# A decoder layer on one core: the projections' 64-row group as 128 high-and-low columns in four passes

## The chip, the cores and the metric

The kernel runs on one core of a Trainium2 chip. The metric is the device time of one execution in microseconds. Engines: TensorE (PE in the profile, its weight load PEld), VectorE (DVE), ScalarE (ACT), GpSimd (POOL), SyncE (SP, which here issues all DMAs).

## The reference, cut to what matters

Four batches of 1024 tokens with 256 features go through a linear attention of rank 64, a cross attention and a feed-forward network in a 4-bit grid. The change lies in the first of them:

```python
Q = x @ WQ.T;  K = x @ WK.T;  invQ = Q @ Winv.T;  invK = K @ Winv.T
z = jnp.cumsum(x, axis=1) / counts
fwd_r = Q @ V_b * jnp.cumsum(K @ W_b, axis=1)
inv_r = jnp.cumsum(invK @ V_b, axis=1) * (invQ @ W_b)
tri_r = Q @ V_t * jnp.cumsum(K @ W_t, axis=1) * (z @ X_t)
out = (fwd_r @ U_b.T + 0.5 * inv_r @ U_b.T + 0.5 * tri_r @ U_t.T + biases) / counts
```

## The kernel before

Products in full precision are made of two parts of each factor: a high part (rounded, type fp32r) and a low part (the rest). `mm_parts` (L1031 to L1033) makes three matmuls of them: high by high, high by low, low by high.

The 256x256 weights are folded into seven column groups of R = 64 in the preparation: `proj_h` and `proj_l` are [128, 2, 7 * 64]. The columns 6R to 7R are those of invQ @ W_b. A half batch of 512 tokens (`q` = 0 to 7) is projected by `proj_tiles`: groups t = 0, 1, 2 give 128 rows each, t = 3 gives 64. Each has two contraction steps `k`, so 6 matmuls of 512 columns. Group 0 and 2 go to PSUM bank 6, groups 1 and 3 to bank 7 (other banks in the preparation).

VectorE takes them: `bi_half` (L1535 and the scan L1528) for groups 0 and 1, and `tri_half` for groups 2 and 3. `tri_half` scans group 2, multiplies its lower 64 rows with group 3 (L1543, which reads PSUM), the upper 64 with the inverse counts (L1545), and adds or multiplies both into `ranks` (L1548, L1550). `y_half` (L1149) multiplies `ranks` with the output weights, and `x1_half` (L1558) adds that to X.

The order on every engine is written out by hand; engines wait for one another by counting semaphores. `s_proj` counts the groups that TensorE made, `s_proj_used` what VectorE took of them, `s_tri` the finished `ranks`. After a preparation (up to about 51 us), which also projects batch 0, the function `batch(b, more)` runs for b = 0 to 3: it does the cross attention of batch b in steps i = 0 to 9 (tiles of 128 queries), and with `more` (b = 0 to 2) the linear attention of batch b + 1 between them. On TensorE step i = 3 projects groups 0 and 1 of the first half of b + 1, i = 4 groups 2 and 3, i = 5 makes the output product and turns the second normed half, i = 6 projects its groups 0 and 1, i = 7 its groups 2 and 3, i = 8 makes the second output product. In i = 4 VectorE has the maximum of tile 4, `tri_half`, two `gate_tile` (gz, L1574), `raw_scales` (for the feed-forward weights) and `mix_tile` of tile 2; in i = 5 the maximum of tile 5, `x1_half`, `mix_tile` of tile 3, `raw_rounder`, and `xnT_low` (the low half of the turned normed input, L1498), which the projections of i = 6 wait for. `mix_tile` makes dmix (L1590), which frees the PSUM bank of the next PV product (`pv_tile`, L1228 and L1230). In i = 7 VectorE has `tri_half`, `mix_tile` of tile 5 and, for b = 0 and 1, the statistics of two batches ahead. GpSimd's operations in these steps are additions and products of SBUF tiles: `bias_half` (L486), `sum_half` (L502), `base_tiles` (L509, L513) and those on the raw weights, which first wait for VectorE's `wsc`. Then a loop over 32 tiles does the feed-forward network.

## Time and profile before

| | us |
|---|---|
| median of three runs | 545.34 (544.75 to 546.62) |
| the profiled execution | 544.99 |
| its span | 543.2 |
| PE busy | 523.3 (96%) |
| PEld busy | 455.9 (84%) |
| DVE busy | 449.6 (83%) |
| ACT busy | 343.2 (63%) |
| POOL busy | 409.6 (75%) |

The profile is one execution. Busy time is a sum of instructions; matmuls overlap each other, so their step from start to start says more than their duration. The views used are the page (parts by number), the timeline (instructions of one engine in order of time; in brackets how long the engine stood idle before it and what ended that), groups by source line, and windows (busy time of each engine in a stretch, with TensorE's granted clock as a share of full speed).

### The profile page before, as it was taken

The numbers are of one execution on the slowest core, as the hardware profiler recorded it, in microseconds if no ns is written. First come the engines' busy times: TensorE is split into PE (matmuls) and PEld (weight loads), VectorE is DVE, ScalarE is ACT, GpSimd is POOL, SyncE is SP. The second block draws the span as 40 slices with busy tenths as digits, with TensorE's granted clock in tenths as the row PEclk, the third lists the DMA queues.
The fourth block names the chain that finished last, engine by engine and source line by source line (L and its number), as shares of the span: only waits on it lengthen the run. The fifth ranks groups of instructions, "written<-read, shape, count | busy, mean of one in ns | idle before, by whom it ended". The sixth has DMA issues, their size and how long they took to land.

```text
span 543.2 us, 10677 instructions
## 1 busy us (share of the span) xinstructions
PE 523.3 (96%) x3089; PEld 455.9 (84%) x3089; DVE 449.6 (83%) x1118; ACT 343.2 (63%) x811; POOL 409.6 (75%) x639
## 2 busy tenths in 40 slices
PE   7998899999999999999999998999999999999997
PEld 4876688888888888888888887898899999999996
DVE  3688579786797957978679779998899999999986
ACT  3555544747446266553486666887778888888763
POOL 4156938949769499498796938889988888888864
PEclk9998999999999999999999999999999999999999
DMA  8621300000000000000000000000000000000001
GB/s 245 190 89 48 113 1 1 1 2 1 1 1 0 2 1 1 2 0 2 1 2 1 0 1 1 1 19 20 19 20 20 19 19 19 20 24 24 21 19 49
DMA packets 16130, 13.86 MB, mean 26 GB/s; under 512 B 3883, under 2 KB 15839, under 8 KB 16095
## 3 DMA queue, kind: packets, MB, share of 16 engines
q1 hardware_dynamic: 16095, 13.43, 8.1%
q8 instruction: 17, 0.28, 0.2%
q14 instruction: 18, 0.15, 0.1%
HBM read 9.23 MB, written 4.19 MB: 25 GB/s over the span
## 4 chain that ended last, share of the span: by engine, by line
PE 70%; DVE 15%; issue 7%; ACT 5%; POOL 2%; DVEq 0%; ACTq 0%; POOLq 0%
PE ps L1031 16%; PE ps L1033 15%; PE ps L1032 15%; PE ps L1230 10%; PE ps L1410 3%; PE ps L1218 2%; PE ps L1228 2%; ACT xn_sums L714 1%; PE ps L1149 1%; DVE X L1558 1%; DVE gz L1574 1%; PE ps L1278 1%; PE ps L1121 1%; DVE parts L1498 1%; DVE st L1562 1%
## 5 line engine op out<-in xcount | busy, mean ns | idle before, releaser
L1031 PE MATMUL ps<-keys_h,nT_h 128*128 128x256 f32 (+6 forms) x272 | 85.9, 316 | 2.7 <-DVE keys_l L1498 1.9
L1033 PE MATMUL ps<-keys_h,nT_l 128*128 128x256 f32 (+6 forms) x272 | 83.1, 306 | 0.0
L1032 PE MATMUL ps<-keys_l,nT_h 128*128 128x256 f32 (+6 forms) x272 | 83.1, 306 | 0.0
L1031 PE MATMUL ps<-parts,xq_parts 128*128 128x512 f32 (+1 forms) x192 | 74.5, 388 | 0.0
L1033 PE MATMUL ps<-parts,xq_parts 128*128 128x512 f32 (+1 forms) x192 | 72.0, 375 | 0.0
L1032 PE MATMUL ps<-parts,xq_parts 128*128 128x512 f32 (+1 forms) x192 | 71.7, 373 | 0.0
L1230 PE MATMUL ps<-V,probT 128*128 128x256 f32 x288 | 67.4, 379 | 0.0
L757 ACT ACTIVATE prob<-ps,nbias 128x205 f32<-128x205 f32 (+7 forms) x32 | 25.7, 804 | 60.7 <-DVE nbias L1580 60.6
L1230 PEld LDWEIGHTS ps<-V,probT 128*128 128x128 f32 x288 | 54.5, 189 | 7.7
L1031 PEld LDWEIGHTS ps<-keys_h,nT_h 128*128 128x128 f32 x272 | 51.3, 188 | 7.1 <-DVE keys_l L1498 2.3
L1032 PEld LDWEIGHTS ps<-keys_l,nT_h 128*128 128x128 f32 x272 | 51.4, 189 | 3.3
L631 POOL TENSOR_TENSOR probT<-prob,probT 128x704 f32<-128x704 f32 x31 | 47.5, 1533 | 8.3 <-ACT probT L831 8.3
L1033 PEld LDWEIGHTS ps<-keys_h,nT_l 128*128 128x128 f32 x272 | 51.4, 189 | 1.6
L633 POOL TENSOR_TENSOR probT<-probT 128x704 f32<-128x704 f32 x31 | 47.7, 1540 | 2.4
L520 POOL TENSOR_TENSOR pool_carrier<-powers 128x1 f32<-128x1 f32 x70 | 15.0, 214 | 45.4 <-DVE wsc L1615 27.8
L1696 DVE TENSOR_TENSOR prob<-prob,ps 128x256 f32<-128x256 f32 (+1 forms) x96 | 37.6, 393 | 12.6 <-ACT prob L815 12.4
L829 ACT ACTIVATE probT<-prob 128x704 bf16<-128x704 f32 x31 | 24.5, 791 | 28.4 <-DVE prob L1715 28.3
L1580 DVE TENSOR_REDUCE nbias<-ps 128x1 f32<-128x205 f32 (+7 forms) x32 | 26.4, 826 | 17.5 <-PE ps L1202 17.5
L1498 DVE TENSOR_TENSOR nT_l<-ps,nT_h 128x768 fp32r<-128x768 f32 (+2 forms) x49 | 40.7, 845 | 0.1
L1033 PEld LDWEIGHTS ps<-parts,xq_parts 128*128 128x128 f32 x192 | 36.0, 188 | 5.4
L1032 PEld LDWEIGHTS ps<-parts,xq_parts 128*128 128x128 f32 x192 | 36.2, 188 | 4.6
L1031 PEld LDWEIGHTS ps<-parts,xq_parts 128*128 128x128 f32 x192 | 36.1, 188 | 4.3
(236 smaller groups left out, 1595.4 us busy)
## 6 DMA issues: line engine op xcount, KB each, us to landing
X<-in_x_dram SPq DMA_DIRECT2D x8, 512.0 KB, 4.4
out_dram<-X SPq DMA_DIRECT2D x32, 128.0 KB, 1.7
early<-in_L_ffn_w_down_dram SPq DMA_DIRECT2D x1, 704.0 KB, 6.7
early<-in_L_ffn_w_gate_dram SPq DMA_DIRECT2D x1, 640.0 KB, 4.5
early<-in_L_ffn_w_up_dram SPq DMA_DIRECT2D x1, 640.0 KB, 5.7
ctx_rows<-in_ctx_dram SPq DMA_DIRECT2D x1, 308.0 KB
early<-in_L_attn_Winv_dram SPq DMA_DIRECT2D x1, 256.0 KB, 3.9
early<-in_L_attn_WQ_dram SPq DMA_DIRECT2D x1, 256.0 KB, 4.6
```

What stands on the lines that cost most here:

```text
L631: g.tensor_tensor(ht, hy, hm, ALU.add).then_inc(s_h_added, 1)
L633: g.tensor_tensor(ht, ht, hm, ALU.subtract).then_inc(s_h_rounded, 1)
L757: a.activation(prob[:, i % 2, CTX0:L], flat[:, CTX0:L], ACT.Exp, bias=nbias[:, i:i + 1], scale=1.0, accum_out=rsum[:, i:i + 1]).then_inc(s ...
L829: a.activation(hsq, hy, ACT.Square, scale=GRID_SLOPE).then_inc(s_hsq, 1)
L1031: mm(o, wh, mh, start=start, stop=False, **kw)
L1032: mm(o, wh, ml, start=False, stop=False, **kw)
L1033: return mm(o, wl, mh, start=False, stop=stop, **kw)
L1230: last = mm(ps[:, 5, 0:D], probT[:, i % 2, m, :], V[:, m - 1, :], start=False, stop=(m == i + 1))
L1410: last = turn(ps[:, 5 + k // 4, (k % 4) * P:(k % 4 + 1) * P], hq_wide[:, k * P:(k + 1) * P], ident[:])
L1498: return v.tensor_tensor(o, whole, high.bitcast(F32), ALU.subtract)
L1580: v.tensor_reduce(nbias[:, i:i + 1], flat[:, CTX0:(i + 2) * P], AX.X, ALU.max, negate=True).then_inc(s_neg_max, 1)
L1696: v.tensor_tensor(hh[:, lo:lo + width], sg[:, lo:lo + width], ps[:, c, width:2 * width], ALU.mult).then_inc(s_hh, 1)
```

## The change

In the preparation the low part of the seventh column group is written behind its high part, as an eighth group of `proj_h`. For t = 3 TensorE then makes, in each of the two contraction steps, one matmul with these 128 columns (high and low) and the high part of the input, into 128 rows of the bank, and one with the 64 high columns and the low part of the input, added into the lower 64 rows: four matmuls in place of six. ScalarE copies the upper 64 rows to a new tile `inv_q` (`inv_q_low`, called at i = 4 and 7 and twice in the preparation), VectorE adds the lower 64 rows to it, and L1543's operation reads `inv_q` in place of PSUM. Two semaphores are new. In `tri_half` the product with the inverse counts now comes ahead of these.

```diff
--- before.py
+++ after.py
@@ -119,6 +119,7 @@
         fwd_tri = sb("fwd_tri", [P, HTOK])
         inv_z = sb("inv_z", [P, HTOK])
         ranks = sb("ranks", [P, S])
+        inv_q = sb("inv_q", [R, HTOK])
         st2 = sb("st2", [P, HALF, 6])
         mv2 = sb("mv2", [P, TPB, 2])
         sm = sb("sm", [P, 11, TPB])
@@ -180,7 +181,7 @@
 
 
 
-        xnT_h, xnT_l, proj_h, proj_l, att_h, att_l = rooms(parts, HTOK, HTOK, 7 * R, 7 * R, D, D)
+        xnT_h, xnT_l, proj_h, proj_l, att_h, att_l = rooms(parts, HTOK, HTOK, 8 * R, 7 * R, D, D)
         gwT_h, gwT_l = rooms(xq_parts, D, D)
 
         xn1 = hid[:, HALF:TPB, :]
@@ -269,6 +270,8 @@
         s_proj_used = sem("proj_used")
         s_zE = sem("zE")
         s_tri = sem("tri")
+        s_inv_q = sem("inv_q")
+        s_inv_q_sum = sem("inv_q_sum")
         s_biased = sem("biased_input")
         s_att_w = sem("attention_weights")
 
@@ -740,6 +743,13 @@
                                         scale=sm[:, 1, i:i + 1])
                 last.then_inc(s_hid, 1)
 
+            def inv_q_low(q, bank=6):
+
+                act.wait_ge(s_proj, q * 4 + 4)
+                if not (isinstance(q, int) and q == 0):
+                    act.wait_ge(s_inv_q_sum, q)
+                a.activation(inv_q[:], ps[R:2 * R, bank + 1, :], ACT.Copy).then_inc(s_inv_q, 1)
+
             def gate_tile(b, i):
                 act.wait_ge(s_gz, b * TPB + (i + 1))
                 act.wait_ge(s_base, b * TPB + (i + 1))
@@ -836,6 +846,8 @@
                         exp_tile(b, i)
                     if 1 <= i <= TPB:
                         turn_tile(b, i - 1)
+                    if more and i in (4, 7):
+                        inv_q_low(b * 2 + (2 + i // 7))
                     if more and i in (2, 5):
                         xnT_half(b * 2 + (2 + i // 5), i // 5)
                     if i == (1 if is_first(b) else 0):
@@ -910,6 +922,7 @@
                 act.wait_ge(s_xn_turned, 2 + (j + 1))
                 a.activation(xnT1_h[:, :, j * 2 * P:(j + 1) * 2 * P],
                              ps[:, j, :].rearrange("p (k n) -> p k n", k=KD), ACT.Copy).then_inc(s_xnT_h, 1)
+            inv_q_low(0, 4)
             act.wait_ge(prep_mm, 4)
             a.activation(out_w[:], ps[:, 2, 0:D], ACT.Copy)
             a.activation(bias_row[:], ps[:, 2, D:2 * D], ACT.Copy).then_inc(prep_ev, 1)
@@ -924,6 +937,7 @@
             last.then_inc(s_att_w, 1)
             act.wait_ge(prep_mm, 7)
             a.activation(gwT_h, ps[:, 2, :].rearrange("p (j n) -> p j n", j=KD), ACT.Copy).then_inc(prep_ev, 1)
+            inv_q_low(1, 4)
             norm2_half(0, 0)
             act.wait_ge(prep_mm, 8)
             for m in range(KD):
@@ -1129,11 +1143,17 @@
                         pe.wait_ge(s_xnT_l, q * 2 + 2)
                     if t >= 2 and banks[0] == banks[2]:
                         pe.wait_ge(s_proj_used, q * 4 + (t - 1))
-                    m = R if t == 3 else P
                     for k in range(KD):
-                        c = slice(t * P, t * P + m)
-                        last = mm_parts(ps[0:m, banks[t], :], (proj_h[:, k, c], proj_l[:, k, c]),
-                                        (xT[0][:, k, :], xT[1][:, k, :]), start=(k == 0), stop=(k == KD - 1))
+                        c = slice(t * P, (t + 1) * P)
+                        if t < 3:
+                            last = mm_parts(ps[:, banks[t], :], (proj_h[:, k, c], proj_l[:, k, c]),
+                                            (xT[0][:, k, :], xT[1][:, k, :]), start=(k == 0), stop=(k == KD - 1))
+                        else:
+
+                            mm(ps[:, banks[t], :], proj_h[:, k, c], xT[0][:, k, :], start=(k == 0), stop=False,
+                               skip_group_check=True)
+                            last = mm(ps[0:R, banks[t], :], proj_h[:, k, 6 * R:7 * R], xT[1][:, k, :], start=False,
+                                      stop=(k == KD - 1), skip_group_check=True)
                     last.then_inc(s_proj, 1)
 
             def y_half(b, h):
@@ -1538,12 +1558,14 @@
 
                 c = slice(h * HTOK, (h + 1) * HTOK)
                 scan(q, h, scan_rest, bank, 3)
-                ve.wait_ge(s_proj, q * 4 + 4)
                 ve.wait_ge(s_proj_used, q * 4 + 3)
-                v.scalar_tensor_tensor(inv_z[0:R, :], scan_rest[0:R, :], alphas[0:R, 0:1], ps[0:R, bank + 1, :], ALU.mult,
-                                       ALU.mult).then_inc(s_proj_used, 1)
                 v.tensor_tensor(inv_z[R:2 * R, :], scan_rest[R:2 * R, :], inv_row[R:2 * R, c], ALU.mult).then_inc(s_zE, 1)
+                ve.wait_ge(s_inv_q, q + 1)
+                v.tensor_tensor(inv_q[:], ps[0:R, bank + 1, :], inv_q[:], ALU.add).then_inc(s_proj_used, 1)
                 ve.wait_ge(s_proj_used, q * 4 + 4)
+                v.scalar_tensor_tensor(inv_z[0:R, :], scan_rest[0:R, :], alphas[0:R, 0:1], inv_q[:], ALU.mult,
+                                       ALU.mult).then_inc(s_inv_q_sum, 1)
+                ve.wait_ge(s_inv_q_sum, q + 1)
                 ve.wait_ge(s_y, b * TPB)
                 v.tensor_tensor(ranks[0:R, c], fwd_tri[0:R, :], inv_z[0:R, :], ALU.add)
                 ve.wait_ge(s_zE, q + 1)
@@ -1829,8 +1851,8 @@
             ve.wait_ge(prep_ev, 1)
             for m in range(KD):
                 low(pairs_of(proj_l[:, m, 0:4 * R]), bilinear_sums(m), pairs_of(proj_h[:, m, 0:4 * R]))
-                low(pairs_of(proj_l[:, m, 3 * R:7 * R])[:, :, R:2 * R], trilinear_sums(m),
-                    pairs_of(proj_h[:, m, 3 * R:7 * R])[:, :, R:2 * R])
+            low(proj_l[:, :, 4 * R:5 * R], ps[:, 0:KD, 2 * R:3 * R], proj_h[:, :, 4 * R:5 * R])
+            low(proj_h[:, :, 7 * R:8 * R], ps[:, 0:KD, 5 * R:6 * R], proj_h[:, :, 6 * R:7 * R])
             low(proj_l[:, :, 5 * R:6 * R], xt[:], proj_h[:, :, 5 * R:6 * R]).then_inc(prep_v, 1)
             ve.wait_ge(w_in[2], 16 * 7)
             v.tensor_scalar(ub2[:, :, R:2 * R], ut[:], alphas[:, 1:2], None, ALU.mult)
```

## Rows read from the trace of the kernel before

**Rows 1.** Page, part 4: the chain that ended last, share of the span by engine.

```profile
PE 70%; DVE 15%; issue 7%; ACT 5%; POOL 2%; DVEq 0%; ACTq 0%; POOLq 0%
```

**Rows 2.** Timeline of PE, batch 0, first half (start us, us, engine line op tiles).

```profile
75.22 0.40 PE L1031 MATMUL ps<-parts 128*64 128x512 f32 x1
...
76.61 0.28 PE L1031 MATMUL ps<-xq_parts,nT_h 128*128 128x256 f32 x1
```

**Rows 3.** Timeline of DVE, same stretch, tri_half and what follows.

```profile
75.42 1.22 DVE L1528 TENSOR_TENSOR_SCAN xn_sums<-ones,ps 128x512 f32<-128x512 f32 x1 [1.04 <-PE ps L1033]
76.81 0.74 DVE L1543 SCALAR_TENSOR_TENSOR inv_z<-xn_sums,alphas,ps 64x512 f32<-64x512 f32 x1 [0.16 <-PE ps L1033]
77.58 0.69 DVE L1545 TENSOR_TENSOR inv_z<-xn_sums,inv_row 64x512 f32<-64x512 f32 x1
78.30 0.68 DVE L1548 TENSOR_TENSOR ranks<-fwd_tri,inv_z 64x512 f32<-64x512 f32 x1
79.72 0.88 DVE L1574 SCALAR_TENSOR_TENSOR gz<-ps,sm,gate_row 128x256 f32<-128x256 f32 x2
```

**Rows 4.** Timeline of DVE, low half of the next normed input.

```profile
91.93 1.28 DVE L1498 TENSOR_TENSOR parts<-ps,parts 128x512 fp32r<-128x512 f32 x2
```

**Rows 5.** Timeline of PE, the two places that follow VectorE in the first half.

```profile
87.17 1.06 PE L1121 MATMUL ps<-ident,xn_sums 128*128 128x128 f32 x8 [0.29 <-DVE X L1558]
...
92.86 0.28 PE L1033 MATMUL ps<-xq_parts,nT_l 128*128 128x256 f32 x1
...
93.26 0.50 PE L1031 MATMUL ps<-parts 128*128 128x512 f32 x1
```

**Rows 6.** Timeline of PE, batch 0, second half: PV product of tile 7.

```profile
119.16 0.60 PE L1228 MATMUL ps<-ctx_rows,probT 77*128 77x256 f32 x2
```

**Rows 7.** Timeline of DVE, batch 0, second half: tri_half's end, dmix of tile 6.

```profile
107.44 1.10 DVE L1548 TENSOR_TENSOR ranks<-fwd_tri,inv_z 64x512 f32<-64x512 f32 x1
...
108.55 1.27 DVE L1550 TENSOR_TENSOR ranks<-fwd_tri,inv_z 64x512 f32<-64x512 f32 x1
...
118.33 0.48 DVE L1590 SCALAR_TENSOR_TENSOR dmix<-ps,rinv,th 128x256 f32<-128x256 f32 x1
```

**Rows 8.** Timelines of DVE and PE, the same two places in batch 2.

```profile
258.66 0.48 DVE L1590 SCALAR_TENSOR_TENSOR dmix<-ps,rinv,th 128x256 f32<-128x256 f32 x1
...
261.19 0.60 PE L1228 MATMUL ps<-ctx_rows,probT 77*128 77x256 f32 x2
```

**Rows 9.** By source line: ScalarE's 64-row copy, VectorE's L1676 (ns min/median/max).

```profile
L906 ACT ACTIVATE inv_row<-ps x2: 582/588/595, 17.2 to 17.7; 64x512 f32<-64x512 f32 x2
L1676 DVE SCALAR_TENSOR_TENSOR nrm<-nrm,ps x29: 406/408/414, 320.7 to 509.4; 128x256 f32<-128x256 f32 x29
L1676 DVE SCALAR_TENSOR_TENSOR nrm<-nrm,xs x3: 620/817/936, 281.8 to 303.4; 128x256 f32<-128x256 f32 x3
```

**Rows 10.** Timeline of POOL, batch 0, first half.

```profile
82.86 0.19 POOL L520 TENSOR_TENSOR pool_carrier<-powers 128x1 f32<-128x1 f32 x1 [8.66 <-DVE wsc L1615]
```

**Rows 11.** Timeline of POOL, batch 0, second half.

```profile
108.54 1.86 POOL L513 TENSOR_TENSOR X<-X,hid 128x256 f32 x2
```

**Rows 12.** Timelines of DVE, POOL and PE in the preparation, in order of time.

```profile
25.45 0.69 DVE L1550 TENSOR_TENSOR ranks<-fwd_tri,inv_z 64x512 f32<-64x512 f32 x1
...
25.72 0.47 POOL L520 TENSOR_TENSOR pool_carrier<-powers 128x1 f32<-128x1 f32 x1 [13.79 <-ACT bias_row L915]
...
27.09 1.89 PE L1149 MATMUL ps<-out_w,ranks 128*128 128x256 f32 x8
...
32.88 0.69 DVE L1498 TENSOR_TENSOR xq_parts<-ps,xq_parts 128x512 fp32r<-128x512 f32 x1 [0.40 <-ACT xq_parts L926]
...
51.47 0.42 PE L1031 MATMUL ps<-keys_h,nT_h 128*128 128x334 f32 x1 [0.82 <-ACT prob L757]
```

**Rows 13.** Windows of 1 us: busy of each engine, then PEclk, DMA share, GB/s.

```profile
45.00:46.00 1.00, 0.00 (x0) 0.00 (x0) 1.00 (x6) 0.39 (x1) 0.77 (x4) 1.00 0.00 0
...
47.00:48.00 1.00, 1.00 (x7) 0.95 (x7) 0.96 (x5) 0.76 (x3) 0.99 (x2) 0.54 0.09 16
```

## The prediction

> **What bounds the kernel now.** I read the views in this order. First the page's chain of work that ended last [rows 1]: TensorE carries 70% of it, VectorE 15%. So the kernel is near TensorE's limit, but a sixth of the end is set by VectorE, and the question is whether the edited step lies in that sixth. Then the timelines around the 64-row group. In batch 0 the six 64-row matmuls run from 75.22 to 76.61 [rows 2]: 1.39 / 6 = 0.232 us from start to start. VectorE meanwhile scans group 2, which it had waited for, and then does four dependent 64x512 operations [rows 3]; the step from L1545 to L1548, both from SBUF alone, is 78.30 - 77.58 = 0.72 us. From that scan on, VectorE has no idle time up to the end of the next low half of the normed input, 91.93 + 1.28 = 93.21 [rows 4], and TensorE starts the next projections 0.05 us later, at 93.26 [rows 5]. Its last gate matmul began at 92.86, and one of 256 columns takes 0.12 us from start to start (estimated as half of 0.232), so it was free at 92.98 and stood 0.28 us; at 87.17 it stood for VectorE too, for X of L1558 [rows 5]. Batches 1 and 2 repeat this pattern, so it stands three times in the trace. Thus the first half of each `more` batch is set by VectorE from group 2's end on. The second half is different: there the next place where TensorE needs VectorE is the PV product of tile 7, at 119.16 [rows 6], which needs dmix of tile 6, done at 118.33 + 0.48 = 118.81 [rows 7]; slack 0.35, less 0.05 for the signal. Batch 2's second half has more: 258.66 + 0.48 = 259.14 against 261.19 [rows 8], because two batches ahead there is nothing left to norm.
>
> **The change part by part.**
>
> TensorE. Two of six matmuls go in each of eight half batches, 16 x 0.232 = 3.7 us [rows 2], and group 3 ends 0.46 us earlier each time. Group 2's end does not move. That four passes cost four times 0.232, although half of them load 128 columns and half 64, is read from the same rows: 128- and 64-column matmuls follow each other without a longer step. What the trace does not show is a switch at every pass; its bounds are 0 and one more step of 0.232 per group, and I take 0 since both switches of the present group show nothing; even 0.232 would be hidden where VectorE decides. The Trainium skill, TensorEngine Tiling (Array Packing), Key Properties, says that a change of tiling mode drains the engine; if a 64-column pass counts as such a mode, that speaks against the change, but the present switches show no drain, and by either the sum stays within the bounds just given.
>
> ScalarE. A 64x512 copy from PSUM takes 582 to 595 ns [rows 9], so 8 x 0.59 = 4.7 us. It waits for group 3, at i = 4 and 7. Queued behind it at i = 4 are the tanh of tiles 4 and 5, which need gate products that TensorE makes after group 3 anyway; at i = 7 it is the turning copy of tile 7, likewise made later. In the preparation the second copy stands ahead of norm2_half(0, 0), and who needs that one's turned output is VectorE's nT_low, queued behind the second tri_half, which waits for the same copy. Cost 0 in these places. Is the copy in time for VectorE's add? The old L1543 began at 76.81; group 3 now ends 0.46 before that, 76.35, the copy at 76.94, and the add is due only after L1545, at 76.81 + 0.72 = 77.53. Yes, by 0.6 us. In the second half ScalarE is still copying tile 6 then, and I allow 0.1 us.
>
> VectorE. The product L1545 goes first, then comes the new add (PSUM and SBUF, 64x512), then L1543's operation with both tensors in SBUF, then L1548 and L1550. One more dependent operation: I take 0.72 us by L1545's step; the other end is 0.77, the step 76.81 to 77.58 [rows 3]. The low halves of the weights in the preparation change their slices, not their number or element count: 0.
>
> First halves, batches 0 to 2: VectorE's run from the scan to 93.21 is 0.72 longer, and TensorE's start at 93.26 moves by all of it; its own 0.46 only lengthens its standing. GpSimd is idle meanwhile (8.66 us until wsc, [rows 10]), so nothing is slowed. 3 x 0.72 = +2.2.
>
> Second halves, batches 0 and 1: here GpSimd's X minus hid runs beside VectorE from 108.54 [rows 11], and L1548 and L1550, both with two SBUF sources, take 1.10 and 1.27 us [rows 7] where L1545 took 0.69 [rows 3]. With L1543 reading SBUF only, there are three such operations in the stretch; GpSimd ends at 110.40, so the last one is relieved. I take 0.72 + 0.1 (copy) + 0.2 (contention) = 1.0. dmix then ends at 119.8, TensorE's PV at 119.86: +0.7 each, +1.4. Bounds 0.4 (0.72 alone: 118.81 + 0.72 + 0.05 - 119.16) and 1.1 each. Batch 2: 259.14 + 1.0 is before 261.19 - 0.46 = 260.73, so here the saving counts: -0.46.
>
> Preparation, two half batches. VectorE ended L1550 at 25.45 + 0.69 = 26.14 and TensorE began the output product L1149 at 27.09 [rows 12], busy up to then. Now TensorE arrives at 26.63, VectorE at 26.86. But GpSimd's bias additions wait for bias_row, which comes 0.46 after fewer matmuls, so they start at 25.72 - 0.46 = 25.26 and run beside L1548 and L1550, which now lie 0.72 later (25.47 on). By [rows 7] against [rows 3] that adds 0.4 + 0.6 = 1.0: output product at 27.9, +0.84. From there TensorE runs through to the turned gate weights; ScalarE copies them, and VectorE's low half waits for that copy at 32.88 [rows 12]. From 32.88 VectorE is busy with no idle time until the first maximum, whose exponential TensorE waits for at 51.47 [rows 12]; in that run lies the second tri_half, +0.72. Together +1.5; without contention 26.86 + 0.05 - 27.09 + 0.72 = +0.5. I take 1.5, since all four GpSimd additions fall in the stretch.
>
> Batch 3 and the feed-forward loop have no edited step and shift as a whole. Sum: 1.5 + 2.2 + 1.4 - 0.5 = +4.6 us. Against the profiled execution, 544.99, that is 549.6; the median of the three runs lies 0.35 above it, so 549.9. With the low ends 0.5 + 2.2 + 0.8 - 0.5 = +3.0 (548.3), with the high ends 1.6 + 2.3 + 2.2 - 0.2 = +5.9 (551.2).
>
> **The rivals.**
>
> (a) TensorE sets everything and VectorE's 0.72 is absorbed: -3.7, 541.6. For it: TensorE's share of the chain [rows 1]. Against it: the idle-free VectorE run that ends 0.05 us before TensorE's start, in all three batches, and the standing at 87.17.
>
> (b) Only the first halves and the preparation lose, and in the second halves the chain to dmix of tile 6 has more room than I read (from an order of waits that the records don't show): 0.5 + 2.2 - 3 x 0.46 = +1.3, 546.6. It decides where VectorE gains more than 0.7 us before 118.33.
>
> (c) L1543's operation becomes slow since both its sources now lie in SBUF. Nearest rows: L1676, 128x256, 408 ns with one source in PSUM and 620 to 936 ns with both in SBUF [rows 9]. Taking the lowest, +0.21 for 256 columns, +0.42 for 512, at seven places where VectorE decides: +2.9, 552.8. Against it: those three ran beside GpSimd's operations, as L1548 did. The Trainium skill, Vector Engine (DVE) Microarchitecture Reference, Points that are easy to get wrong, says that such an operation with two SBUF sources that aren't bf16 runs at half rate; this would be the same mechanism. No row shows it undisturbed.
>
> (d) The clock. At 45 to 46 TensorE is not busy at all, and at 47 to 48 its granted clock is 0.54, towards the 1.2 GHz level [rows 13]; VectorE's run hides that now. TensorE's standing before the second output product (about 40 us) grows by about 0.7. If the clock falls there already, the 12 matmuls of 512 columns for the keys take 0.232 more each, +2.8: 552.7.
>
> (e) The saving does not come, since the fused pass takes longer or the sequence stays at six steps: then VectorE's part is the same and batch 2 loses its -0.46: 550.4, inside the range.
>
> **How the numbers follow.** About 0.3%, 1.6 us, is what a measurement of this kernel can tell from no change, so "same" is 543.7 to 547.0. My sum, with (e) in it, has 0.62; (a) 0.08, (b) 0.12, (c) 0.12, (d) 0.06. Faster is (a), 0.08; same is (b), 0.12; slower is the rest, 0.80. The predicted time is 549.9. The range goes down to (b) and up to (c) and (d), 546.4 to 552.9, which leaves out (a) and the outer ends of (c) and (d), no more than 2 in 10.
>
> **What would show it.** TensorE's group 3 in four matmuls, next work 0.46 us sooner after group 2. VectorE from the scan's start to that of gz, L1574, 79.72 - 75.42 = 4.3 us before [rows 3], now 5.0 in first halves. TensorE standing before the turns of the normed input and before the projections 0 and 1 in every first half, longer by 0.7 to 1.2. In second halves a new standing before the PV product of tile 7, named as waiting for dmix, in batches 0 and 1 and not in 2. The first exponential's follower at about 53.0 rather than 51.47. The forecast is wrong if the stretch from group 2's end to the next projections has the same length as before, or if L1543's operation, undisturbed, takes over 0.8 us.

## The result, and the profile after

| | before | after |
|---|---|---|
| median | 545.14 (544.75 to 546.62, 4 runs) | 551.29 (549.80 to 551.39, 4 runs) |
| the profiled execution | 544.99 | 551.25 |
| its span | 543.2 | 549.5 |
| PE busy | 523.3 (96%) | 521.0 (95%) |
| DVE busy | 449.6 (83%) | 456.7 (83%) |
| ACT busy | 343.2 (63%) | 347.9 (63%) |

The changed kernel is slower: ratio 1.0093, 95% interval 1.0071 to 1.0115, which is 3.9 to 6.3 us. Predicted were 549.9 us with a range of 546.4 to 552.9. The executions of either kernel lie in groups some 1.5 us apart (the kernel before on another chip: 8 of 19 runs at 544.96 to 545.44, the others at 546.51 to 548.11). Of the four runs above, one of the kernel before lies above its lower group and three of the changed one do, so the 6.15 us between the medians hold some luck; what the groups come from is taken up at the end of the experiments.

The lines of `tri_half` have new numbers: scan L1548, the product with the inverse counts L1562, the new addition L1564, L1543's operation L1566, the two rank operations L1570 and L1572, dmix L1612. The fused passes are L1153 and L1155, `mm_parts` L1045 to L1047, the output product L1169, the turns of the normed input L1135.

The page of after, part 4 (the chain that ended last, as [rows 1]):

```profile
PE 59%; DVE 22%; issue 8%; ACT 8%; POOL 1%; DVEq 0%; ACTq 0%; POOLq 0%
```

TensorE's share fell from 70% to 59%, VectorE's rose from 15% to 22%: work was taken from the engine that mostly sets the end and given to one that sets it in places. Where it does so is in the view of TensorE's waits between 62 and 345 us (line that waited, what for: us in total, times, longest). Before:

```profile
PE ps L1121 <- DVE X L1558: 0.9, 3, 0.3
PE ps L1031 <- DVE gz L1574: 0.5, 1, 0.5
```

and after:

```profile
PE ps L1135 <- DVE X L1580: 4.1, 3, 1.4
PE ps L1248 <- DVE dmix L1612: 1.5, 2, 0.8
PE ps L1045 <- DVE gz L1596: 1.0, 3, 0.5
```

The first line is the standing before the turns of the normed input, once in every first half (0.3 us each before, 1.4 now). The second did not exist before: the PV product of tile 7 waits for dmix of tile 6, in two batches of three.

How far the second trace runs behind the first can be followed by the starts of the 32 PV products, L1228 before and L1248 after. The delay is 2.31 us at the first one (62.62 to 64.93), so the preparation gave this. From tile 1 of one batch to tile 1 of the next it grows to 3.97, 5.65 and 6.12 us; within batch 3 it stays at 6.12 to 6.13. Split at tile 4, the three first halves gave 0.62, 0.58 and 0.57 us, the second halves 1.03, 1.10 and -0.10.

**TensorE's part came as forecast.** Timeline of PE of after, batch 0, first half, and further on the turns:

```profile
77.55 0.40 PE L1153 MATMUL ps<-parts 128*128 128x512 f32 x1
77.79 0.39 PE L1155 MATMUL ps<-parts 128*64 128x512 f32 x1
78.02 0.39 PE L1153 MATMUL ps<-parts 128*128 128x512 f32 x1
78.24 0.39 PE L1155 MATMUL ps<-parts 128*64 128x512 f32 x1
...
90.09 1.06 PE L1135 MATMUL ps<-ident,xn_sums 128*128 128x128 f32 x8 [1.35 <-DVE X L1580]
```

Four passes in place of six, 0.22 to 0.24 us from start to start, with 128 and 64 columns in turn and nothing between them. The 0.46 us saved reappear at L1135 as standing, 1.35 us in place of the 0.29 of [rows 5].

**VectorE, undisturbed.** Timeline of DVE of after, same stretch, to be held against [rows 3]:

```profile
77.75 1.22 DVE L1548 TENSOR_TENSOR_SCAN xn_sums<-ones,ps 128x512 f32<-128x512 f32 x1 [1.04 <-PE ps L1047]
79.01 0.69 DVE L1562 TENSOR_TENSOR inv_z<-xn_sums,inv_row 64x512 f32<-64x512 f32 x1
79.73 0.68 DVE L1564 TENSOR_TENSOR inv_q<-ps,inv_q 64x512 f32<-64x512 f32 x1
80.45 0.74 DVE L1566 SCALAR_TENSOR_TENSOR inv_z<-xn_sums,alphas,inv_q 64x512 f32<-64x512 f32 x1
81.22 0.68 DVE L1570 TENSOR_TENSOR ranks<-fwd_tri,inv_z 64x512 f32<-64x512 f32 x1
81.92 0.69 DVE L1572 TENSOR_TENSOR ranks<-fwd_tri,inv_z 64x512 f32<-64x512 f32 x1
82.64 0.88 DVE L1596 SCALAR_TENSOR_TENSOR gz<-ps,sm,gate_row 128x256 f32<-128x256 f32 x2
```

From the scan to gz it is 82.64 - 77.75 = 4.89 us, before it was 4.30.

**VectorE beside GpSimd.** The second half of batch 0, as [rows 7]; first DVE, then POOL, then the PE product that waits:

```profile
108.80 0.77 DVE L1562 TENSOR_TENSOR inv_z<-xn_sums,inv_row 64x512 f32<-64x512 f32 x1
109.68 0.68 DVE L1564 TENSOR_TENSOR inv_q<-ps,inv_q 64x512 f32<-64x512 f32 x1
110.40 0.98 DVE L1566 SCALAR_TENSOR_TENSOR inv_z<-xn_sums,alphas,inv_q 64x512 f32<-64x512 f32 x1
111.42 1.25 DVE L1570 TENSOR_TENSOR ranks<-fwd_tri,inv_z 64x512 f32<-64x512 f32 x1
112.69 1.14 DVE L1572 TENSOR_TENSOR ranks<-fwd_tri,inv_z 64x512 f32<-64x512 f32 x1
...
122.35 0.48 DVE L1612 SCALAR_TENSOR_TENSOR dmix<-ps,rinv,th 128x256 f32<-128x256 f32 x1
```

```profile
108.98 1.86 POOL L512 TENSOR_TENSOR hid<-hid,th 128x256 f32<-128x256 f32 x2
...
111.39 1.88 POOL L516 TENSOR_TENSOR X<-X,hid 128x256 f32 x2
```

```profile
122.89 0.70 PE L1248 MATMUL ps<-ctx_rows,probT 77*128 77x256 f32 x2 [0.76 <-DVE dmix L1612]
```

The same three operations that took 0.74, 0.68 and 0.69 us take 0.98, 1.25 and 1.14 here. The addition, which has one source in PSUM, keeps its 0.68.

**The preparation.** Windows of after around the first logits (us, busy time and count of PE, PEld, DVE, ACT, POOL, then TensorE's granted clock, DMA share, GB/s):

```profile
48.00:49.00 1.00, 1.00 (x11) 0.99 (x10) 0.96 (x10) 1.00 (x3) 1.00 (x2) 1.00 0.06 16
...
51.00:52.00 1.00, 0.00 (x0) 0.00 (x0) 1.00 (x5) 0.43 (x3) 0.92 (x3) 1.00 0.00 0
...
53.00:54.00 1.00, 1.00 (x6) 0.77 (x5) 0.00 (x0) 0.75 (x2) 1.00 (x2) 0.50 0.51 160
54.00:55.00 1.00, 1.00 (x4) 0.47 (x4) 0.51 (x1) 0.43 (x1) 1.00 (x3) 0.50 1.09 388
```

and of before:

```profile
48.00:49.00 1.00, 1.00 (x6) 1.00 (x7) 1.00 (x10) 1.00 (x3) 0.84 (x6) 0.50 0.00 0
...
53.00:54.00 1.00, 1.00 (x9) 0.79 (x8) 0.27 (x1) 0.81 (x5) 1.00 (x2) 1.00 1.07 376
54.00:55.00 1.00, 1.00 (x11) 1.00 (x10) 0.00 (x0) 1.00 (x4) 1.00 (x3) 1.00 1.11 342
```

In both traces TensorE has a stretch of 3 to 4 us at the lower level, 1.2 GHz (0.50). Before, it lay at 47 to 51 us, where TensorE is early and VectorE's run decides. After, it lies at 52 to 56 us, in the logits of tile 1 and the turns behind them, which TensorE alone sets. Their start came 52.15 - 51.47 = 0.68 us later. This execution had begun a little sooner, though: VectorE's first low half of the projection weights (called the first low half below) starts at 14.92 and not at 15.14, so from there it is 37.23 us against 36.33, and the change made the way 0.90 us longer. From the logits to the first PV product it is 64.93 - 52.15 = 12.78 us against 62.62 - 51.47 = 11.15, so in this pair of executions the clock costs 1.63 us.

### The profile page after: what moved, and what is told of

Same layout as the page of the kernel before. It is cut to its first block, busy times and chain, and to the rows that moved or that the text cites. A ratio compares the mean times of both kernels' runs of the same rounds, so it can differ in the third digit from the quotient of the medians.

```text
span 549.5 us, 10660 instructions
## 1 busy us (share of the span) xinstructions
PE 521.0 (95%) x3073; PEld 454.1 (83%) x3073; DVE 456.7 (83%) x1126; ACT 347.9 (63%) x819; POOL 410.3 (75%) x639
## 4 chain that ended last, share of the span: by engine, by line
PE 59%; DVE 22%; issue 8%; ACT 8%; POOL 1%; DVEq 0%; ACTq 0%; POOLq 0%
PE ps L1045 13%; PE ps L1047 13%; PE ps L1046 13%; PE ps L1250 6%; PE ps L1430 3%; DVE X L1580 2%; ACT xn_sums L717 1%; DVE st L1509 1%; PE ps L1248 1%; DVE xn_sums L1548 1%; PE ps L1238 1%; DVE st L1584 1%; DVE nT_l L1518 1%; DVE dmix L1612 1%; DVE nbias L1602 1%
## 5 line engine op out<-in xcount | busy, mean ns | idle before, releaser
L1045 PE MATMUL ps<-keys_h,nT_h 128*128 128x256 f32 (+6 forms) x272 | 86.1, 316 | 4.3 <-ACT prob L767 2.4
L1047 PE MATMUL ps<-keys_h,nT_l 128*128 128x256 f32 (+6 forms) x272 | 83.4, 307 | 0.0
L1045 PE MATMUL ps<-parts,xq_parts 128*128 128x512 f32 (+1 forms) x192 | 74.6, 388 | 0.0
L1047 PE MATMUL ps<-parts,xq_parts 128*128 128x512 f32 (+1 forms) x192 | 72.0, 375 | 0.0
L1045 PEld LDWEIGHTS ps<-keys_h,nT_h 128*128 128x128 f32 x272 | 51.5, 189 | 8.6 <-ACT prob L767 2.6
L1047 PEld LDWEIGHTS ps<-keys_h,nT_l 128*128 128x128 f32 x272 | 51.5, 189 | 1.7
L1718 DVE TENSOR_TENSOR prob<-prob,ps 128x256 f32<-128x256 f32 (+1 forms) x96 | 37.6, 392 | 12.7 <-ACT prob L825 12.5
L1047 PEld LDWEIGHTS ps<-parts,xq_parts 128*128 128x128 f32 x192 | 36.0, 188 | 5.4
L1045 PEld LDWEIGHTS ps<-parts,xq_parts 128*128 128x128 f32 x192 | 36.2, 188 | 4.3
```

The lines of the kernel that those rows point to most:

```text
L1045: mm(o, wh, mh, start=start, stop=False, **kw)
L1047: return mm(o, wl, mh, start=False, stop=stop, **kw)
L1718: v.tensor_tensor(hh[:, lo:lo + width], sg[:, lo:lo + width], ps[:, c, width:2 * width], ALU.mult).then_inc(s_hh, 1)
```

## The experiments

My theory after the two traces: (1) the addition makes VectorE's run longer by 0.6 us at each half, (2) in second halves three operations with both sources in SBUF are stretched by GpSimd's work, (3) in the preparation 0.7 us is VectorE's and 1.6 us the place of the low-clock stretch, (4) TensorE's saving is worth nothing where VectorE decides. The rivals: the loss is in the fused passes or the copy; operations with two SBUF sources are slow in any case; TensorE's shorter group is a gain that something else eats.

The ratios in this part stand against runs of the kernel before made in between on the same chip; its median there was 546.54 (19 runs) for the first four kernels, 546.67 (26 runs) for the next four and 545.38 (17 runs) for the last two.

**The clock.** The changed kernel, with eight matmuls of no use behind the first two gate products of batch 0:

```diff
+                    if i == 0 and is_first(b):
+                        keep_warm(8, 5)
```

> The changed kernel with eight 512-column bf16 matmuls of identity by identity (their result is not read, they fill the bank of the PV products) in step 0 of batch 0, behind the gate products of tiles 0 and 1, where TensorE stood 2.38 us. Theory (the clock fell in that standing and the next 3.5 us ran at the 1.2 GHz level, which cost 2.31 - 0.68 = 1.6 us): 549.6, the PV product of tile 0 of batch 0 begins at about 63.3 instead of 64.93, and the granted clock from 52 to 56 us is 1.00. Rival (the 1.6 us come from later waits for ScalarE or VectorE, the low clock is only seen beside them): 551.2, the PV product stays at 64.9.

Measured: 550.63 us (550.20 to 551.44, 4 runs), ratio 1.0079 (1.0047 to 1.0110). The profiled run (550.54) had the granted clock 1.00 in every window from 40 to 66 us, and from the first logits to the first PV product it took 64.27 - 53.12 = 11.15 us, as before. That logits start at 53.12 and not at 52.15 is not the edit's: this execution was 0.97 us late already at VectorE's first low half, 15.89 against 14.92 us. So the 1.63 us between the two profiles are the clock's. The runs don't show a gain: the interval overlaps that of the changed kernel (1.0071 to 1.0115), and the two medians, 0.66 us apart, belong to series in which the kernel before had 545.14 and 546.54. An execution starts earlier or later by up to 1 us, and the last section shows that the stretch does not fall on the same matmuls in each.

**The saving alone.** The kernel before with four passes, no copy and no addition; the low part of the weights is left out of invQ @ W_b:

```diff
-                    m = R if t == 3 else P
...
+                            mm(ps[:, banks[t], :], proj_h[:, k, c], xT[0][:, k, :], start=(k == 0), stop=False,
+                               skip_group_check=True)
+                            last = mm(ps[0:R, banks[t], :], proj_h[:, k, 6 * R:7 * R], xT[1][:, k, :], start=False,
+                                      stop=(k == KD - 1), skip_group_check=True)
```

> TensorE's part alone: the 64-row group in four passes, but no copy and no add, VectorE takes the lower 64 rows from PSUM as before; the product of the group's low weights with the input is left out of the result. Theory: nothing is gained in the three first halves, where VectorE decides; 0.46 in the preparation, 0.46 in the second half of batch 2, at most 0.30 in those of batches 0 and 1: -1.5 us, 543.6. Rival (TensorE sets everything): -3.7, 541.4.

Measured: 545.69 us (543.88 to 547.25, 10 runs), ratio 0.9984 (0.9967 to 1.0002), that is -1.8 to +0.1 us: the rival's -3.7 is out, the forecast -1.5 is not. The profiled run had a low clock twice, at 52 to 57 and 59 to 64 us (2.99 us late at the first PV product), so the trace is read from there: the delay falls to 2.28 us at the end, -0.71 in all, and -0.41 of that is batch 2's second half. In the first halves it falls by 0.46 and comes back by 0.39; TensorE's waits tell where:

```profile
PE ps L1121 <- DVE X L1564: 2.1, 3, 0.7
```

Against 0.9 us before: of each 0.46 us saved in the group, 0.4 us is now standing for X. So of the 2.8 us of work that the six half batches behind the preparation save, 0.7 comes through, most of it where VectorE is not late. In the preparation the saving shows once more: from the first low half to the first logits it is 35.89 us against 36.33.

**The addition alone.** Six passes as before, ScalarE's copy multiplied by zero, and the addition:

```diff
-                a.activation(inv_q[:], ps[R:2 * R, bank + 1, :], ACT.Copy).then_inc(s_inv_q, 1)
+                a.activation(inv_q[:], ps[0:R, bank + 1, :], ACT.Copy, scale=0.0).then_inc(s_inv_q, 1)
```

> ScalarE's and VectorE's part alone: TensorE makes the 64-row group in six passes as before; ScalarE copies its 64 rows times zero to inv_q and VectorE adds that, so every added instruction and wait of the change is there. Theory (VectorE sets the first halves and, for the longer tri_half, the second ones too, so TensorE's saving is worth little beside it): 551.2 to 552.0, at most 0.7 us above the changed kernel. Rival (the saving of 16 x 0.232 = 3.7 us was had in full and the rest cost over 9 us): 555.0.

Measured: 551.90 us (550.18 to 553.30, 4 runs), ratio 1.0089 (1.0055 to 1.0123), which can't be told from the changed kernel's. The profiled run (553.30) had a granted clock of 0.50 from 54 to 57 us and 0.72 on the mean of 60 to 66. From its first PV product on, the first halves give 0.60 us each (4.12 to 4.72, 5.84 to 6.44, 7.55 to 8.14), the second halves 1.12, 1.10 and 0. So the loss in the halves needs no fused pass; it is the copy's and the addition's.

**GpSimd's share.** The changed kernel, with `base_tiles` of tiles 6 and 7 held back until `tri_half` of the second half is done:

```diff
+                if more:
+                    pool.wait_ge(s_tri, b * 2 + 4)
```

> The changed kernel with one wait more: in the second halves GpSimd begins the products and subtractions of tiles 6 and 7 only when VectorE has finished tri_half, so they don't run beside it. Theory (contention for SBUF stretched the three operations with two SBUF sources to 0.98, 1.25 and 1.14 us): they take 0.74, 0.68 and 0.69 us, 1.26 less; TensorE's standing before the PV product of tile 7 goes, about -1.1 us each in batches 0 and 1, -0.4 in batch 2: 548.6. Rival (they are slow for another reason, such as two SBUF sources by themselves): their durations stay, and the added wait costs up to 1 us: 551.2 to 552.5.

Measured: 547.77 us (546.97 to 549.05, 10 runs), ratio 1.0031 (1.0013 to 1.0049). Timeline of DVE and of POOL, batch 0, second half (lines here are two higher than in after):

```profile
109.87 0.68 DVE L1566 TENSOR_TENSOR inv_q<-ps,inv_q 64x512 f32<-64x512 f32 x1
110.59 0.74 DVE L1568 SCALAR_TENSOR_TENSOR inv_z<-xn_sums,alphas,inv_q 64x512 f32<-64x512 f32 x1
111.37 0.68 DVE L1572 TENSOR_TENSOR ranks<-fwd_tri,inv_z 64x512 f32<-64x512 f32 x1
112.07 0.69 DVE L1574 TENSOR_TENSOR ranks<-fwd_tri,inv_z 64x512 f32<-64x512 f32 x1
```

```profile
112.92 1.61 POOL L512 TENSOR_TENSOR hid<-hid,th 128x256 f32<-128x256 f32 x2 [3.67 <-DVE ranks L1574]
```

All three are back at their undisturbed times, and the second halves cost -0.17, -0.13 and -0.44 us (read by the PV products) in place of 1.03, 1.10 and -0.10. The first halves stay at 0.57. One wait takes 2.8 us off the three second halves. That is more than the change lost there, for the kernel before has contention in them too, and no run holds GpSimd back in it. The Trainium skill says in GPSIMD Engine Reference, Specifications, that GpSimd shares its SBUF interfaces with VectorE and that they collide in instructions of VectorE with two SBUF inputs; this trace agrees, with 0.98 against 0.74, 1.25 against 0.68 and 1.14 against 0.69 us.

**Two sources in SBUF or one.** The changed kernel, the sum written to PSUM:

```diff
-                v.tensor_tensor(inv_q[:], ps[0:R, bank + 1, :], inv_q[:], ALU.add).then_inc(s_proj_used, 1)
+                v.tensor_tensor(ps[0:R, bank + 1, :], ps[0:R, bank + 1, :], inv_q[:], ALU.add).then_inc(s_proj_used, 1)
```

> The changed kernel with one edit: VectorE's addition writes the sum back into the group's bank of PSUM, so that the operation behind it (the alphas' multiply and add, L1566) has one source in SBUF again, as in the kernel before. Theory (operations with both sources in SBUF are stretched while GpSimd works, and only then): undisturbed nothing changes, 0.74 us for L1566 either way; in the second halves of batches 0 and 1, where L1566 took 0.98 us beside GpSimd, it takes 0.74 to 0.77, while the two rank operations behind it stay above 1.1 us. That is 2 x 0.24 = 0.5 us: 550.8 us. Rival (L1566 lasts longer for the mere order of work, or VectorE's second source from PSUM is as exposed as one from SBUF): L1566 stays at 0.95 or more in second halves, 551.3 us.

Measured: 549.49 us (547.97 to 551.12, 10 runs), ratio 1.0044 (1.0027 to 1.0061). Timeline of DVE and of POOL, batch 0, second half:

```profile
110.64 0.74 DVE L1566 SCALAR_TENSOR_TENSOR inv_z<-xn_sums,alphas,ps 64x512 f32<-64x512 f32 x1
111.42 0.68 DVE L1570 TENSOR_TENSOR ranks<-fwd_tri,inv_z 64x512 f32<-64x512 f32 x1
112.11 1.12 DVE L1572 TENSOR_TENSOR ranks<-fwd_tri,inv_z 64x512 f32<-64x512 f32 x1
```

```profile
111.60 2.23 POOL L516 TENSOR_TENSOR X<-X,hid 128x256 f32 x2 [0.15 <-issue]
```

L1566 took 0.74 us beside GpSimd, as the theory had it; that L1570 would stay above 1.1 us was wrong. Since L1566 was done sooner, L1570 had begun before GpSimd's next operation (111.42 against 111.60), and now GpSimd's was the one stretched: 2.23 us for two in place of 1.88. So the profiled gain was 0.24 + 0.57 us in this half, 0.8 where 0.24 was forecast. Undisturbed, in the first half, the operation takes 0.74 us with both sources in SBUF (after) and 0.74 us with one in PSUM (before and here).

**Moving the upper rows to GpSimd.** GpSimd makes the two products of the upper 64 rows (L1545 and L1550) in batches 1 to 3, first in the kernel before, then in the changed one, then with the extra matmuls too:

```diff
+                pool.wait_ge(s_proj_used, q * 4 + 3)
+                g.tensor_tensor(inv_z[R:2 * R, :], scan_rest[R:2 * R, :], inv_row[R:2 * R, c], ALU.mult).then_inc(s_zE, 1)
...
+                g.tensor_tensor(ranks[R:2 * R, c], fwd_tri[R:2 * R, :], inv_z[R:2 * R, :], ALU.mult).then_inc(s_upper, 1)
```

> The kernel before with GpSimd making the upper 64 rows' two products (L1545 and L1550) in batches 1 to 3, and everything else as it was. VectorE's run of a first half gets 1.4 us shorter. Theory (in the kernel before, TensorE stands only 0.28 and 0.45 us for VectorE in a first half, and nearly nothing in a second): a first half gives back at most 0.7 us, three of them 2.1, and the second halves give nothing or lose some tenths, since GpSimd was working there anyway: 543.5 us, between 542.8 and 545. Rival (VectorE's run sets the halves in full, so that what it loses comes back in full): 6 x 1.4 = 8 us, 537. Second rival (GpSimd is slower at these products and VectorE waits for it at the next half): 546 or more.

Measured: 543.95 us (542.22 to 545.39, 6 runs), ratio 0.9952 (0.9925 to 0.9978), the one kernel here that beats both. In its trace the delay to the kernel before goes from -0.04 to -0.98, -1.89 and -2.79 us: each first half gives 0.9 us, more than the 0.73 us of standing that I had counted, and each second half nothing.

> The changed kernel with the same edit: GpSimd makes the upper 64 rows' two products (L1562 and L1572) in batches 1 to 3. That takes 1.4 us from a VectorE run that the change made 0.6 us longer. Theory (the change loses by VectorE's run at every half, and TensorE's shorter group shows once that run is covered): first halves go from +0.6 to about -0.45 against the kernel before, second halves from +1.1 to about -0.45; the preparation's 2.3 us stay, for batch 0 is not touched: 545.1 + 2.3 - 3 x 0.45 - 3 x 0.45 = 544.7 us; with a share of the second halves lost to GpSimd, up to 546.5. Rival (the loss sits in TensorE or in the copy, not in VectorE's length): 551 us. Second rival (GpSimd takes over as what ends last): above 549.

Measured: 549.83 us (548.29 to 551.37, 9 runs), ratio 1.0054 (1.0036 to 1.0072), where 544.7 to 546.5 were expected. A miss, and the timelines of DVE and POOL in the first half tell why:

```profile
78.05 0.68 DVE L1590 TENSOR_TENSOR inv_q<-ps,inv_q 64x512 f32<-64x512 f32 x1 [0.40 <-ACT inv_q L771]
78.77 0.79 DVE L1592 SCALAR_TENSOR_TENSOR inv_z<-xn_sums,alphas,inv_q 64x512 f32<-64x512 f32 x1
79.59 1.65 DVE L1596 TENSOR_TENSOR ranks<-fwd_tri,inv_z 64x512 f32<-64x512 f32 x1
```

```profile
77.73 1.28 POOL L529 TENSOR_TENSOR inv_z<-xn_sums,inv_row 64x512 f32<-64x512 f32 x1 [2.53 <-DVE xn_sums L1570]
79.17 1.53 POOL L532 TENSOR_TENSOR ranks<-fwd_tri,inv_z 64x512 f32<-64x512 f32 x1 [0.15 <-POOL inv_z L529]
```

Of the 1.4 us taken from VectorE, 0.40 is spent standing for ScalarE's copy, which the product L1562 had covered, and 0.97 on L1596, which runs beside GpSimd's product and takes 1.65 us in place of 0.68. The first halves gave 0.52, 0.49 and 0.55 us, nearly as in after, the second ones 0.49, 0.55 and -0.44. I had counted GpSimd's idle time as free, and left out that the edit itself ends it at the moment VectorE's two-source operation runs. In the kernel before the same edit had L1548's operation at 0.98 us, not 1.65, and no copy to wait for.

> The kernel of the run before this one with a few matmuls more behind the first two gate products of batch 0, so that TensorE does not stand idle before the first logits. Theory (1.6 us of the changed kernel's preparation are a stretch at the lower of the two granted clocks that had lain under VectorE's run): the stretch at 1.2 GHz is gone in the profile, and the median falls by 0.7 to 1.6 us against the kernel without these matmuls: 543.6 us. Rival (the clock falls elsewhere instead, or the added matmuls delay the logits): no less than without, 544.7 or more.

Measured: 549.12 us (548.19 to 549.52, 10 runs), ratio 1.0044 (1.0027 to 1.0062). A gain of 0.7 us in the median over the run before it, the low end of the forecast, but the two intervals overlap, and the absolute forecast of 543.6 fell with the run before it. The other part of the forecast, no stretch at 1.2 GHz in the profile, failed. The extra matmuls kept the clock at 1.00 up to 60 us, and then it fell all the same:

```profile
62.00:63.00 1.00, 1.00 (x4) 0.81 (x3) 0.10 (x1) 0.00 (x0) 0.86 (x3) 0.50 0.00 0
```

From the first logits to the first PV product it is 65.12 - 52.43 = 12.69 us, 1.5 us more than in the run before it, whose profiled execution (548.29), without the extra matmuls, had its stretch at 48 to 52 us, under VectorE's run, and took 11.15. This is the rival: the clock fell elsewhere instead.

**The preparation and the halves apart.** The fused passes, copy and addition for batch 0 alone (`q < 2`), and for batches 1 to 3 alone (`q >= 2`); elsewhere six passes with the same low weights, and the old `tri_half`:

```diff
+                        if t == 3 and not (q < 2):
+                            w = proj_h[:, k, 6 * R:7 * R], proj_h[:, k, 7 * R:8 * R]
+                            last = mm_parts(ps[0:R, banks[t], :], w, (xT[0][:, k, :], xT[1][:, k, :]),
+                                            start=(k == 0), stop=(k == KD - 1))
```

> The fused passes, the copy and the addition for batch 0 alone; batches 1 to 3 have six passes and no addition, as in the kernel before. Theory (the change's loss in the preparation is 0.7 us of VectorE's run and the rest is where the lower granted clock falls, which varies from run to run in the kernel before too): against the median of the kernel before on this chip +0.7 to +1.5 us; in the profile TensorE's first logits of batch 0 start 0.7 us after those of the kernel before when the start-up is taken off, and from the first output product of batch 0 on the distance to the kernel before is constant. Rival (the change moves the stretch at 1.2 GHz from behind VectorE's run to behind the logits in every run): +2.3 us in the median too.

Measured: 547.49 us (545.77 to 549.03, 12 runs), ratio 1.0021 (1.0002 to 1.0040), 2.1 us above the kernel before in the median. The median alone would be the rival's number, but the ratio of the runs, 0.1 to 2.2 us, does not decide between the two. Three of the twelve runs lie at 545.8 to 545.9, 0.9 us above the lower group of the kernel before (544.8 to 545.7), nine at 547.4 or more; the rival's "in every run" falls by these three. The profiled run (548.03) has the stretch at 52 to 57 us, and its first PV product 2.45 us late. With the start-up taken off, its first logits come 0.92 us after those of the kernel before, where 0.7 was expected. The distance then stays at 2.45 to 2.47 up to tile 6, but grows to 3.03 us in batch 0's second half, where no edited instruction runs; a constant distance was expected. Timeline of DVE there, line numbers of this kernel:

```profile
109.16 1.31 DVE L1577 TENSOR_TENSOR inv_z<-xn_sums,inv_row 64x512 f32<-64x512 f32 x1
110.50 1.24 DVE L1580 TENSOR_TENSOR ranks<-fwd_tri,inv_z 64x512 f32<-64x512 f32 x1
111.76 1.13 DVE L1582 TENSOR_TENSOR ranks<-fwd_tri,inv_z 64x512 f32<-64x512 f32 x1
```

The GpSimd product that runs beside L1577, first here, then in the kernel before together with VectorE's operation there:

```profile
109.20 0.72 POOL L512 TENSOR_TENSOR hid<-hid,th 128x256 f32<-128x256 f32 x1
```

```profile
106.69 0.71 DVE L1545 TENSOR_TENSOR inv_z<-xn_sums,inv_row 64x512 f32<-64x512 f32 x1
106.81 1.18 POOL L509 TENSOR_TENSOR hid<-hid,th 128x256 f32<-128x256 f32 x1
```

The same two operations meet in both kernels. Before, GpSimd's was the one stretched (1.18 us) and VectorE's took 0.71; here GpSimd's takes 0.72 and VectorE's 1.31. VectorE's operation started 0.12 us ahead of the product before and 0.04 us ahead here. What contention costs, and whom, thus hangs on less than 0.1 us in how the two engines' work happens to lie, and a late preparation alone shifted it.

> The fused passes, the copy and the addition for batches 1 to 3 alone; batch 0 has six passes and no addition. Theory (the halves of batches 0 to 2 lose 0.62 + 1.05, 0.58 + 1.1 and 0.57 - 0.09 us in the profile of the changed kernel, whatever the preparation does): the distance to the kernel before grows by 3.8 us between the first output product of batch 0 and the end, and the median is 3.8 us above that of the kernel before on this chip. Rival (a part of the halves' loss was the late start of the preparation, whose order GpSimd and VectorE kept): 3 us or less.

Measured: 550.61 us (548.90 to 551.23, 6 runs), ratio 1.0082 (1.0053 to 1.0111). In the profile (548.90) the delay is -0.06 us at the first PV product and 3.86 at the last: 3.9 us, as expected, with 0.57, 0.57 and 0.58 in the first halves and 1.08, 1.14 and -0.02 in the second. The median is 5.2 us above that of the kernel before, more than the 3.8 forecast, with an interval of 2.9 to 6.1 us; the two lowest runs (548.90 and 549.05) lie 4.0 us above the lower group of the kernel before. Only one of the six was profiled, so why the upper four lie 1.5 to 2.3 us higher is not shown for this kernel.

**The groups of run times.** The profiles together show what the preparation costs and what is chance:

| profiled execution | first low half to first logits (us) | from there to first PV product (us) | clock below 1.00 between 38 and 68 us |
|---|---|---|---|
| before | 36.33 | 11.15 | 47 to 51 |
| later batches alone | 36.31 | 11.13 | 47 to 51 |
| before, upper rows on GpSimd | 36.31 | 11.14 | nowhere |
| after | 37.23 | 12.78 | 52 to 56 |
| batch 0 alone | 37.25 | 12.77 | 52 to 57 |
| sum in PSUM | 37.23 | 12.80 | 53 to 57 |
| GpSimd held back | 37.26 | 12.51 | 48 to 56 |
| after, upper rows on GpSimd | 37.24 | 11.15 | 48 to 52 |

The first column is the change's: 0.9 us in every execution with it. The second is not clearly so. One and the same preparation took 12.5 to 12.8 us in four executions and 11.15 in a fifth, as its stretch reached past the start of the logits or not. The first three and the last of these executions lie in the lowest group of their kernel's run times, the other four above it, and those of the two kernels of single parts (six passes with the addition, four passes alone), which had two stretches behind the logits and took 3.1 to 3.2 us more, higher still. So the groups seem to go by how often the low clock falls on matmuls that nothing hides. Of the kernel before, over all chips, 38 of 66 runs lie above its lower group, of the five kernels with the changed preparation and no extra matmuls 29 of 45. That the change moves the stretch is therefore not shown; that one profile of my first pair had it hidden and the other exposed can be chance.

## Why the prediction was right, point by point

The sign and its cause hold: VectorE gets a longer run at every half, and TensorE's saving does not pay for it. With the clock's share and the difference in start taken off, the change costs 0.9 in the preparation, 1.8 in the first halves, 2.1 in two second halves and -0.1 in the third, 4.7 us, where 4.6 were forecast. That the two agree so well is luck: the preparation was taken 0.6 and the first halves 0.4 too high, the second halves 0.7 and the third 0.4 too low. The 1.4 us by which the measured median (551.29) lies above 549.9 is in size what one exposed stretch at the low clock costs.

**TensorE.** Held: four steps of 0.23 us, no switch cost, neither by a longer step nor by a drain. Rival (e) falls.

**ScalarE.** Held in the changed kernel: the copy takes 0.59 us at all eight places, no addition waits for it in first halves, and in the second half of batch 0 it costs the addition 0.08 us, where 0.1 was allowed. Only where the product ahead of the addition was taken away did it show, with 0.40 us. That it is free hangs on that cover.

**First halves: +2.2 forecast, +1.8 measured** (0.62, 0.58, 0.57). The step that was off is what the reordering gives back. I wrote that VectorE has no idle time from the scan on, but [rows 3] show it waiting 0.16 us for group 3 between the scan and L1543; with L1562 first and the group done sooner that wait is gone, and the step from the scan to the next operation is 79.01 - 77.75 = 1.26 us in place of 1.39. The addition's own step is 0.72 as taken: 0.72 - 0.13 = 0.59. The run with six passes also has 0.60, so the reordering suffices for it.

**Second halves of batches 0 and 1: +1.4 forecast, +2.1 measured** (1.03 and 1.10, the high bound). VectorE's part was sized about right: from the scan to the end of `tri_half` it takes 6.35 us in batch 0 where it took 5.28, 1.07 longer (1.13 in batch 1), against 1.0 forecast. Inside it the contention was a little under-read, and the reasoning "GpSimd ends at 110.40, so the last one is relieved" failed: GpSimd's work there starts 2.9 us later than before (111.39 against 108.54), as VectorE's does (107.48 against 104.54), so a third operation falls into it. L1566, L1570 and L1572 together are 0.24 + 0.57 + 0.45 = 1.26 us over their undisturbed times, where before L1548 and L1550 were 0.42 + 0.58 = 1.00 over: 0.26 more, and 0.06 more at the product with the inverse counts. The wait before PV of tile 7 is the one forecast, in batches 0 and 1 and not in 2, and up to there each half has lost 0.79 and 0.85 us, against the 0.7 forecast. The step that failed is the slack: I subtracted 0.30 us of room before PV of tile 7 as if it stayed saved. VectorE is still late by the whole 1.0 to 1.1 us behind it, and TensorE pays the rest a little later, standing 0.26 us for gz at the gates of the next batch (131.54 us), where before it did not. The run with GpSimd held back shows that contention is worth more than 1 us in each of these halves, but as it also takes away what the kernel before has, it does not say how much of the change's loss was contention; the rows above say 0.3 of 1.0.

**Second half of batch 2: -0.46 forecast, -0.10 measured.** Room for dmix was read rightly, but the output product was left out: before, VectorE's ranks were ready when TensorE came to it, now it stands for them. From the turns to the output product it is 259.24 - 258.11 = 1.13 us, before it was 253.22 - 252.34 = 0.88. With GpSimd held back, the -0.44 does come.

**Preparation: +1.5 forecast, 0.9 by the change's doing** (2.3 in the first pair of profiles). VectorE's part was forecast at 0.5 to 1.6 and taken at 1.5 (its +0.84 is 0.82 by its own terms). GpSimd's additions did start 0.7 us earlier and did meet L1572 (1.12 us), but L1570 escaped with 0.68. The first `tri_half` ends 1.02 us later by the start of the first low half (26.94 - 14.92 against 26.14 - 15.14), but the low half of [rows 12]'s 32.88 begins only 0.25 later by the same measure (32.91 - 14.92 against 32.88 - 15.14): most of the loss went into the 0.84 us that VectorE had stood for GpSimd's X at 28.96 us before, and stands no more. The second `tri_half` added the rest. The other 1.63 us of the first pair are the clock. Rival (d) had the mechanism and looked for it at one place only: no window from 40 to 46 us is below 1.00. TensorE's stretch at 1.2 GHz was in the rows, 47 to 48 at 0.54, and I wrote that VectorE's run hides it, but did not ask whether it comes at the same place in every execution. Where TensorE works through 47 to 50 us at 2.4 GHz it is done sooner and stands 2.38 us for the first exponential. That the standing brings the low clock behind it is not shown: the kernel before with the upper rows on GpSimd stood 2.38 us too and kept 1.00.

**Rival (a)** falls by the run with the saving alone: at most 1.8 us by its interval in place of 3.7. **Rival (b)** falls by the second halves. **Rival (c)** falls too: with both sources in SBUF the operation takes 0.74 us undisturbed, as with PSUM, so the half rate that the Trainium skill states in Vector Engine (DVE) Microarchitecture Reference, Points that are easy to get wrong, does not show for this operation of 64x512 elements; the 620 to 936 ns of [rows 9] were contention: each of these three operations ended 0.28 to 0.29 us after the end of a GpSimd operation. Part of (c) was real all the same: the same move to SBUF exposed the operation to GpSimd.

## What to carry to other kernels

Before work goes from the bound engine to another one, look in the trace for the places where the first stands for the second: there the saving is worth nothing and the added step counts in full. Ask of an operation not only where its sources lie but who works beside it, and keep one source of VectorE's in PSUM while GpSimd is busy. A wait that slack hides at one place can come back at the next, so follow the late engine until it has caught up. And when one execution is held against another, take off their start and the stretches at the low clock before a difference of 1 to 2 us is put down to the change.

## What was unexpected of the hardware

- An operation of VectorE of 64x512 elements with both sources in SBUF takes 0.68 to 0.74 us alone and up to 1.65 beside GpSimd's; one with a source in PSUM keeps its time (0.68, 0.74). The stretch is no slower pace but a wait for the end of the other's instruction: in all twelve traces every stretched 64x512 operation ended 0.53 to 0.56 us after the end of the GpSimd operation beside it, whether it took 0.77 or 1.65 us (in after, L1562, L1566, L1570 and L1572 by 0.56, 0.54, 0.55 and 0.56). So the price can be estimated as about the time that the GpSimd instruction still has to run. It goes the other way as well: a GpSimd product of 128x256 takes 0.72 us alone and 1.08 to 1.27 behind an operation of VectorE, so which one pays seems to depend on who began. In the run with the sum in PSUM it was GpSimd for L1570; with a lead of 0.04 us (batch 0 alone) the record does not say who was first.
- GpSimd takes 1.28 to 1.69 us for a 64x512 product for which VectorE takes 0.69; still, moving it there made the kernel before 2.7 us faster against its runs on that chip.
- The stretch at 1.2 GHz does not come at the same place in two executions of the same code. The changed kernel and the one with GpSimd held back have one preparation; the second began 0.43 us later (VectorE's first low half at 15.35 against 14.92), and its stretch came almost 4 us sooner and lasted longer. Windows of that kernel:

```profile
48.00:49.00 1.00, 1.00 (x9) 0.98 (x9) 1.00 (x4) 0.61 (x3) 0.92 (x3) 0.88 0.00 0
49.00:50.00 1.00, 1.00 (x7) 1.00 (x6) 0.96 (x10) 1.00 (x4) 0.92 (x5) 0.50 0.06 16
...
52.00:54.00 2.00, 1.39 (x5) 1.39 (x6) 0.78 (x3) 1.90 (x6) 1.92 (x5) 0.50 0.25 52
```

What sets the moment is not settled by these runs.
